# Attention beside a mixture of experts: VectorE's small operations at a unit's start, set one by one behind the first four steps

## What is computed

```python
x = x + attention(xn, W_q, W_k, W_v, W_o) + experts(xn, Wr, Wg, Wu, Wd)
# attention: 16 query heads over 4 key/value heads of 16 dimensions, rotary embedding on Q and K
scores = jnp.einsum('bhqd,bhkd->bhqk', Qr, Kr) / HEAD_DIM ** 0.5
weights = jax.nn.softmax(scores, axis=-1)
out = jnp.einsum('bhqk,bhkd->bhqd', weights, V_rep)
```

## Time and profile before

| | |
|---|---|
| median of 3 runs | 511.3 us (511.15 to 511.53) |
| profiled execution | 511.25 us, its span 509.3 us |
| TensorE busy | 499.2 us, 98% |
| ScalarE busy | 409.5 us, 80% |
| VectorE busy | 368.7 us, 72% |
| GpSimd busy | 172.3 us, 34% |
| granted clock of TensorE | 1.00 |

### The profile page before, as it was taken

One profiled execution on the slowest core, in us unless ns is written; L12 is line 12 of the kernel. 1 busy time (PEld: TensorE's weight loads), 2 busy tenths in 40 slices (PEclk: granted clock), 3 DMA queues, 4 the chain that ended last, 5 costly groups with the idle time before them and its releaser, 6 DMA issues.

```text
span 509.3 us, 10897 instructions
## 1 busy us (share of the span) xinstructions
PE 499.2 (98%) x3904; PEld 275.6 (54%) x3904; DVE 368.7 (72%) x868; ACT 409.5 (80%) x551; POOL 172.3 (34%) x214
## 2 busy tenths in 40 slices
PE   8999999999999999999999999999999999999997
PEld 8836999888888544344444443434334443344433
DVE  4684867977867578888788778888887888873113
ACT  2646776666566699999999999999999999997672
POOL 5007777543530004042742335423444226300000
PEclk9999999999999999999999999999999999999999
DMA  8992467755562132132222034024123212001101
GB/s 289 370 297 68 122 200 233 218 157 149 158 178 68 57 87 61 42 86 85 62 69 80 24 85 125 23 60 112 41 63 96 75 42 72 15 3 33 42 31 63
DMA packets 41428, 52.76 MB, mean 104 GB/s; under 512 B 9792, under 2 KB 27584, under 8 KB 41376
## 3 DMA queue, kind: packets, MB, share of 16 engines
q1 hardware_dynamic: 29152, 34.36, 22.7%
q0 software_dynamic: 3408, 9.31, 7.1%
q10 hardware_dynamic: 8816, 8.40, 4.9%
HBM read 36.18 MB, written 15.60 MB: 102 GB/s over the span
## 4 chain that ended last, share of the span: by engine, by line
PE 94%; ACT 3%; DVE 2%; DMA 1%; issue 0%; ACTq 0%
PE bank L1343 27%; PE bank L1273 14%; PE bank L1333 11%; PE bank L1212 9%; PE bank L1229 9%; PE bank L1283 7%; PE bank L1388 3%; PE bank L1329 3%; PE bank L1173 3%; PE bank L1265 2%; PE bank L1251 2%; ACT xn_t L729 2%; PE bank L1162 1%; PE bank L1222 1%; DMA xs<-in_L_attn_x 1%; PE bank L1177 1%
## 5 line engine op out<-in xcount | busy, mean ns | idle before, releaser
L778 ACT ACTIVATE big<-bank 128x1024 f32<-128x1024 f32 x256 | 249.4, 1024 | 12.1 <-PE bank L1333 11.0
L1343 PE MATMUL bank<-big,v_st 128*32 128x128 f32 (+2 forms) x1584 | 151.3, 454 | 0.0
L1333 PE MATMUL bank<-qs,kb 64*128 64x512 f32 x512 | 130.6, 419 | 0.7 <-ACT big L778 0.7
L978 DVE TENSOR_REDUCE mx<-bank 128x1 f32<-128x512 f32 x128 | 87.8, 686 | 39.6 <-PE bank L1214 38.9
L729 ACT ACTIVATE xn_t<-bank 128x512 f32<-128x512 f32 x128 | 76.5, 597 | 25.9 <-PE bank L1251 14.4
L983 DVE TENSOR_REDUCE mx<-bank 128x1 f32<-128x512 f32 x128 | 87.2, 681 | 13.8 <-PE bank L1229 11.9
L989 DVE CUSTOM_DVE_ANT_0 xn_t<-bank,xn_t 128x512 f32<-128x512 f32 x128 | 87.9, 687 | 1.2
L1333 PEld LDWEIGHTS bank<-qs,kb 64*128 64x128 f32 x512 | 62.6, 184 | 28.6 <-ACT big L778 22.0
L1273 PE MATMUL bank<-xn,work 128*128 128x128 f32 x624 | 76.0, 275 | 0.0
L1273 PEld LDWEIGHTS bank<-xn,work 128*128 128x128 f32 x624 | 72.9, 192 | 0.6 <-issue 0.5
L642 POOL TENSOR_TENSOR xn<-xn,rden 128x256 f32<-128x256 f32 x15 | 9.5, 636 | 165.5 <-DVE rden L1070 149.8
(11 more groups left out here) (147 smaller groups left out, 554.2 us busy)
## 6 DMA issues: line engine op xcount, KB each, us to landing
qs<-q_hl SPq DMA_DIRECT2D x64, 128.0 KB, 2.8
rows_out<-xn ACTq DMA_DIRECT2D x37, 128.0 KB, 2.5
ka<-k_hl SPq DMA_DIRECT2D x64, 64.0 KB
kb<-k_hl SPq DMA_DIRECT2D x64, 64.0 KB, 2.2
xs<-in_L_attn_x SPq DMA_DIRECT2D x4, 512.0 KB, 6.4
big<-in_L_ffn_Wg SPq DMA_DIRECT2D x16, 128.0 KB, 6.4
big<-in_L_ffn_Wu SPq DMA_DIRECT2D x16, 128.0 KB, 6.5
big<-in_L_ffn_Wd SPq DMA_DIRECT2D x16, 128.0 KB, 6.4
```

Source lines behind the costliest of these rows:

```text
L778: act.activation(probs[kt % 2][:, 2 * j:2 * j + 2, :].rearrange("p r q -> p (r q)"), st_ps[j][:, :], ACT.Exp, scale=1.0 / math.sqrt(HD)).t ...
L978: nc.vector.reduce_max(mx[h][:, STEPS + k, 0:1], max_bank(v, i), axis=X_AXIS).then_inc(mx_taken, 1)
L1333: last = mm(out[i], kb[p][half[i], kt // QT, keys], qs[q][half[i], j, :], start=False, stop=True, skip_group_check=kt % QT > 0)
L1343: last = mm(o_ps[32 * r:32 * (r + 1), columns], v_st[p][:, key_block(kt), :], probs[kt % 2][:, r, columns], start=(kt == 0 and columns.sta ...
```

## The change

It is in VectorE's `group` alone. The same operations are issued, in another order. `take_a`, `take_high` and `take_low` of step 0 now come first, and each small piece of work follows the three maxima of a step of its own: `join_maxima` behind step 0, `invert_sums` behind step 1, `split_maxima` behind step 2, `turn_maxima` behind step 3. In the first unit `turn_maxima` stays behind step 0.

```diff
                     for k in range(STEPS):
-                        if k == 0 and not begun:
-                            join_maxima(u + 1, 1 - h)
                         take_a(u + 2, h, k)
                         if k == STEPS - 2 and p == h and not begun:
                             turn_back(g - 1 + h, 1 - h)
                         take_high(u + 2, h, k)
+                        take_low(u + 2, h, k)
                         if k == 0 and not begun:
+                            join_maxima(u + 1, 1 - h)
+                        if k == 1 and not begun:
                             invert_sums(u - 1)
+                        if k == 2 and not begun:
                             split_maxima(u + 1, 1 - h)
-                        take_low(u + 2, h, k)
-                        if k == 0:
+                        if k == (0 if begun else 3):
                             turn_maxima(u + 1, 1 - h)
                     turn_output(u, first and h == 0)
```

## The result

The changed kernel took 508.3 us (median of 5, 508.24 to 508.83) beside 511.3 us of the kernel before: ratio 0.9943, 95% interval 0.9931 to 0.9954, so 3.0 us less. That is in the range, at the upper end of the forecast's own (508.3); of the 3.9 us that were forecast, about three quarters came.

What follows compares the result with a forecast made beforehand. The prediction took attention steps nearly full on TensorE, ScalarE and VectorE, with step 1 lengthened by a late `take_low`. Saving 0.30 us 13 times, other terms nothing, gave -3.9 us: 507.4 us from 511.3; 8-in-10 range 506.7 to 509.8.

Steps and rivals of the forecast that it cites:

- the forecast's own: Range of the main forecast (chance 0.68): 0.28 to 0.34 us a step, up to 0.05 lost in step 4, 506.9 to 508.3 us.
- What bounds it: Attention steps: TensorE busy 98% of the span; the plain step, 2.46 to 2.48 us, nearly full on TensorE, ScalarE and VectorE.
- why step 1 is long: Small VectorE pieces delay `take_low` of step 0, so TensorE's L1222 load waits for L989: 0.30 us of step 1's 2.76.
- (1): Less queued ahead of `take_low` of step 0: step 1 falls to 2.46-2.48 us, 0.30 us saved 13 times, 3.9 us.
- (2), (3): `join_maxima` behind step 0, `invert_sums` behind step 1, `split_maxima` behind step 2: hidden in VectorE's idle time ahead of the next `take_a`.
- (4): `turn_maxima` behind step 3 makes `take_a` of step 4 0.05 us late; taken as nothing, upper bound 0.10 us per step 2 to 4.
- (5): Readers of moved results don't wait: POOL's divide has slack; `load_m` keeps some 7.4 us against at most 3.5 needed.
- The partial case: Rival, chance 0.18: moved operations cost 0.10 us in steps 2 to 4, or step 1 stops at 2.61; 508.7 to 510.0 us.
- The conflict with POOL: Mechanism within the partial rival: `split_maxima` or `turn_maxima` waits for POOL's mixing; a 0.70 us wait costs 1.3 us in all.
- No change: Rival, chance 0.06: step 1's 0.30 us is TensorE's own, the release by L989 a coincidence; 511.3 us.
- slower: Rival, chance 0.05: `load_m` takes over 7.4 us from `turn_maxima`, so L1329 of step 7 waits; at 8 us, 515.2 us.

## Why the prediction was right, and where it was not

- What bounds it, and why step 1 is long: right. Step 1 fell from 2.76 to 2.46 us once `take_low` stood ahead of the small pieces, by that alone, and two thirds of the difference came back when the split was put ahead again (2.67).
- (1): the wait for L989 went, `take_low` was read out 0.22 us into step 1 (0.23 foretold), step 1 shortened by 0.30. What was mis-sized is the term at its end, 0.30 us for each unit: it counted step 1 alone and took step 2 to keep its 2.48. Under "(2), (3)" the prediction expected the steps' lengths as they were, and named it a sign of being wrong if another step takes the time; step 2 took 0.07 to 0.08 of it. Step 2 had been as short only because the long step 1 gave ScalarE time to get ahead. The kernel before shows the plain pair in steps 4 and 5, of which I read step 4 alone (2.46). It even shows steps 1 and 2 as they are without them in front of `take_low`, in the first unit, which has no join, reciprocal or split. By stretches, step 5 of unit 6, and steps 1 and 2 of the first unit:

```profile
308.86:311.41 2.55, 2.55 (x29) 0.98 (x26) 1.99 (x6) 2.52 (x4) 0.62 (x1) 1.00 0.72 205
```

```profile
175.37:177.83 2.46, 2.46 (x29) 0.99 (x26) 1.95 (x5) 2.29 (x4) 0.00 (x0) 1.00 0.02 3
177.83:180.38 2.55, 2.55 (x28) 0.98 (x25) 1.99 (x6) 2.53 (x4) 0.00 (x0) 1.00 0.26 59
```

  So the 5.01 us of the pair could be read off before anything was run.

  The chain through both is ScalarE's, in the changed kernel: the first matmuls of step 1 at 297.41, the gain 0.53 later (297.94), the exponentials 0.50 behind its start (298.44), 1.94 long, TensorE's load 0.05 behind them (300.43), and step 3 1.99 us after that (302.42). Together 5.01 us. No placing of VectorE's pieces that was run made the pair shorter than that; half the gain on ScalarE did (4.93). The term is 5.24 - 5.01 = 0.23 us, not 0.30; times 13 it is 3.0 us, as measured.
- (2), (3): right that the pieces are hidden; step 2's 0.08 us more is not theirs. (4): right to take nothing, step 4 stayed 2.45 to 2.47; its bound was too high, as the earlier trace rows is mostly ScalarE's as well.
- That the total falls on the end of the forecast's own range (508.3) is luck: that end was reckoned from 0.28 us a step and up to 0.05 lost in step 4. What was lost was 0.08 in step 2, for a reason that the prediction did not have.
- (5): right. POOL's wait for the reciprocal stayed long (157.8 us in 13 waits, 149.8 before), and no reader waited for SyncE's load.
- The rivals. The partial case (508.7 to 510.0 us) did not come, though a part only of the saving did. The conflict with POOL is real and missed this kernel by where POOL happens to stand. The row that was held against it, `turn_back` at 0.70 us beside a busy POOL, was no test of it: transposes kept their length in every trace here, the cast and the subtraction of the split did not. "No change" and "slower" didn't come; the latter's price was confirmed by moving `turn_maxima` on.

## What to carry to other kernels

On an engine with a strict order, look for the operation on which another engine waits next, and put it first; where the rest goes matters little so long as it ends before the next such operation is due. When a step becomes shorter, take as its new length not that of one neighbour but of a run of undisturbed steps: what follows a long step may be short because of it. Before a small VectorE operation is moved, see what GpSimd does at its new place.

## What was not expected of the hardware

- Two of VectorE's small operations are stretched while GpSimd works on tensors: L1006 took 0.59 us instead of 0.18 beside one addition of 0.76, L1004 0.70 instead of 0.16 beside another, and one of the two 0.26 to 0.42 beside the multiplications. Where a gather's issue began within L1004 (half the gain), it took up to 0.24. `turn_maxima` (0.20 or 0.21) in more than 100 such meetings, `join_maxima` and `turn_back` never were.
- Beside the multiplications (0.92 us each) the stretched operation ended 0.50 or 0.51 us after the first one's row began, in all 22 cases of the three traces with `invert_sums` put back or the split behind step 3, however late it had started itself. Beside the addition and a copy it ended 0.03 or 0.04 us after theirs. Rows of POOL are rough, so where in its work that moment lies is not shown.
- A small operation's length depends on what stands ahead of it: L1004 takes 0.11 us behind the reciprocal, 0.16 behind `take_high` and 0.17 behind a read-out of the accumulator; `join_maxima` 0.14 behind `turn_output` and 0.18 behind a read-out.
- A matmul's row can start on time while what waits for it starts 0.5 us late, as in step 2 of unit 5 with the reciprocal put back: the idle time of its readers shows it (0.52 us), not its own row.
